# Two blocks of attention and feed-forward: first loads on ScalarE's queue, warm matmuls, and a reordered handover between stages

## The reference

```
x = x + fake_quant(layernorm(x)) @ fake_quant(ctx)   # per batch; 8-bit grid, q1 @ q2
x = x + mx_linear(silu(mx_linear(h, w_gate)) * mx_linear(h, w_up), w_down)   # h = layernorm(x)
x = x + attention(layernorm(x), ctx, ctx, wq, wk, wv, wo)  # 32 query heads, 8 key heads, rope
x = x + ffn(layernorm(x), gate_w, up_w, down_w)            # silu(gate) * up, down
```

## Time and profile before

| | us |
|---|---|
| median of 3 runs | 683.79 |
| lowest, highest | 683.26, 684.01 |
| profiled execution | 685.39 |
| its span, first to last instruction | 683.6 |
| TensorE busy | 661.1 |
| VectorE busy | 516.4 |
| GpSimd busy | 474.2 |
| ScalarE busy | 347.5 |

### The profile page before, as it was taken

How to read it: one execution, slowest core, us unless ns; L and a number is a source line. 1 busy time by engine, 2 the same in 40 slices (tenths; PEclk the granted TensorE clock), 3 DMA queues, 4 the chain that set the end, 5 groups by cost and what they waited for, 6 DMA issues and landing times.

```text
span 683.6 us, 10829 instructions
## 1 busy us (share of the span) xinstructions
PE 661.1 (97%) x3004; PEld 486.5 (71%) x3004; DVE 516.4 (76%) x1024; ACT 347.5 (51%) x667; POOL 474.2 (69%) x435
## 2 busy tenths in 40 slices
PE   6999999999899999999999999999999998999997
PEld 2344444446667888888888888888888776888886
DVE  5999897986788888888888888888888886621113
ACT  2686324424656656656666666666556653221111
POOL 0688958334698788787787787797688477076661
PEclk9999999999999999999999999999999999999999
DMA  8999775403322222232231131131233012013311
GB/s 317 390 328 245 230 198 133 155 1 121 94 78 78 63 85 70 61 89 64 61 99 54 61 105 48 61 107 46 61 94 121 17 32 92 1 48 102 111 63 62
DMA packets 59147, 72.63 MB, mean 106 GB/s; under 512 B 23152, under 2 KB 31472, under 8 KB 58096
## 3 DMA queue, kind: packets, MB, share of 16 engines
q1 hardware_dynamic: 59120, 72.31, 34.5%
HBM read 58.00 MB, written 9.44 MB: 99 GB/s over the span
## 4 chain that ended last, share of the span: by engine, by line
PE 67%; DVE 14%; POOL 8%; issue 7%; ACT 2%; DMA 1%; SPq 1%; DVEq 0%; ACTq 0%; POOLq 0%
PE ps L683 14%; PE ps L685 14%; PE ps L684 14%; PE ps L751 10%; PE ps L716 6%; PE ps L568 3%; PE ps L542 3%; POOL mx_raw L1148 2%; DMA mx_raw<-in_mxw 1%; DVE ps L1578 1%; PE ps L604 1%; POOL mx_w L1157 1%; DVE mx_amax L1406 1%; POOL prob L1220 1%; DVE stats L1319 1%
## 5 line engine op out<-in xcount | busy, mean ns | idle before, releaser
L1220 POOL TENSOR_SCALAR prob<-prob,rinv 128x512 f32<-128x512 f32 x128 | 90.0, 703 | 73.6 <-DVE rinv L1585 73.5
L1046 ACT ACTIVATE prob<-ps,nmax 128x512 f32<-128x512 f32 x128 | 88.5, 691 | 97.2 <-DVE nmax L1578 96.8
L751 PE MATMUL ps<-xt,wq_sb 128*128 128x512 f32 x384 | 103.2, 393 | 3.6 <-DVE q_cos L1593 2.1
L1057 ACT CAST pT<-ps 128x512 fp32r<-128x512 f32 x128 | 75.2, 588 | 53.0 <-PE ps L716 51.9
L1578 DVE CUSTOM_DVE_ANT_0 ps<-ps,mask_sb 128x512 f32<-128x512 f32 x128 | 88.0, 687 | 6.6 <-PE ps L685 6.1
L1599 DVE TENSOR_TENSOR pT<-ps,pT 128x512 fp32r<-128x512 f32 x128 | 86.5, 675 | 3.0 <-ACT pT L1057 2.0
L751 PEld LDWEIGHTS ps<-xt,wq_sb 128*128 128x128 f32 x384 | 71.6, 188 | 22.3 <-issue 4.9
L716 PE MATMUL ps<-idf,prob 128*128 128x128 f32 x512 | 76.8, 272 | 0.4 <-POOL prob L1220 0.3
L716 PEld LDWEIGHTS ps<-idf,prob 128*128 128x128 f32 x512 | 63.6, 140 | 17.8 <-POOL prob L1220 1.6
L683 PE MATMUL ps<-pT,vt 128*128 128x512 f32 x128 | 60.8, 475 | 0.6 <-DVE pT L1599 0.5
L542 PE MATMUL ps<-ctxT,wk_sb 128*128 128x512 f32 x128 | 58.0, 594 | 0.4 <-ACT v_st L892 0.4
(11 more groups left out here) (179 smaller groups left out, 1548.0 us busy)
## 6 DMA issues: line engine op xcount, KB each, us to landing
mx_raw<-in_mxw SPq DMA_DIRECT2D x8, 1024.0 KB, 8.1
wq_raw<-in_wq SPq DMA_DIRECT2D x32, 256.0 KB, 3.2
wo_raw<-in_wo SPq DMA_DIRECT2D x32, 256.0 KB, 2.7
v_scr<-v_st SPq DMA_DIRECT2D x16, 256.0 KB, 3.7
k_scr<-k_st SPq DMA_DIRECT2D x16, 256.0 KB, 3.5
kr<-k_scr SPq DMA_DIRECT2D x16, 256.0 KB, 2.8
kr_swp<-k_scr SPq DMA_DIRECT2D x32, 128.0 KB, 3.4
vr<-v_scr SPq DMA_DIRECT2D x16, 256.0 KB, 3.3
```

Of the source, the lines that this page charges most:

```text
L751: last = mm(query_bank(H), wq_sb[:, par, l, k], xt[:, r, k], start=(n == 0), stop=(n == 11))
L1046: nc.scalar.activation(prob[:, j], bank(j % 2), ACT.Exp, bias=nmax[:, j:j + 1], scale=-1.0, accum_out=rsum[:, j:j + 1]).then_inc(exps, 1)
L1057: copy(pT[:, v % 2, 0, :, i * P:(i + 1) * P], bank(2 + i % 2).rearrange("p (k c) -> p k c", k=4)).then_inc(ph_ready, 1)
L1220: nc.gpsimd.tensor_scalar(prob[:, i], prob[:, i], rinv[:, i:i + 1], 1.0, ALU.mult, ALU.mult).then_inc(probs, 1)
```

## The change

- ScalarE's queue issues the four slices, the first key weights, the rest of the context columns and the second half of the value weights, ahead of its other work. SyncE's queue keeps X, the MX chunks, context rows and all later DMAs.
- TensorE runs eight matmuls of ones (bf16, 512 columns) into the first value bank before `first_values`.
- ScalarE copies the first two value banks before the lifts of chunk 0, and rounds the rows after them.
- The rotation, addition, copy and low part of the two first keys are moved: key 0 behind the MX work on GpSimd and behind the quantisation of the inter products on VectorE, key 1 behind the first steps of query head 0.
- GpSimd splits the weights of heads 2 and 3 in step 0 of units -2 and -1, before the rotation of a query, instead of in step 1.
- Head 3 goes to bank 7, and heads 3 and 4 wait for one rotated head fewer.
- The last late key unit is computed as one quarter before the second stage and three quarters in unit -1, instead of two halves in units -2 and -1.
- `last_low` stands after the first step of `standardise` instead of after five.

The diff, without context lines:

```diff
@@ -62,6 +62,8 @@
+WARM = 8
@@ -112,7 +114,7 @@
-            return bank(7 if isinstance(head, int) and head == 1 else 6)
+            return bank(7 if isinstance(head, int) and head in (1, 3) else 6)
@@ -335,10 +337,6 @@
-            def slice_load(k):
-                sp.dma_start(ctxT[:, k, 0:CTX], ctx_cols[k * P:(k + 1) * P, 0:CTX]).then_inc(ctxT0_in[k], 16)
-                sp.dma_start(wv_sb[:, k, 0:512], wv[k * P:(k + 1) * P, 0:512]).then_inc(wv0_in[k], 16)
@@ -363,20 +361,13 @@
-            slice_load(0)
-            slice_load(1)
-            slice_load(2)
-            slice_load(3)
-            k_load(0)
-            sp.dma_start(ctxT[:, :, CTX:CTOK], ctx_cols[:, CTX:CTOK].rearrange("(k p) c -> p k c", p=P)).then_inc(ctxT1_in, 16)
-            sp.dma_start(wv_sb[:, :, 512:1024], wv[:, 512:1024].rearrange("(k p) c -> p k c", p=P)).then_inc(wv1_in, 16)
@@ -543,6 +534,12 @@
+            def keep_busy():
+                pe.wait_ge(consts_ready, 1)
+                for _ in range(WARM):
+                    mm(bank(rotating(STEPS[0][0][0])), ones[:], ones[:].unsqueeze(1).to_broadcast([P, 4, P]), start=True, stop=True)
@@ -579,6 +576,7 @@
+            keep_busy()
@@ -686,6 +684,7 @@
+            late_keys(4, range(0, 1))
@@ -739,8 +738,7 @@
-                    first = isinstance(H, int) and H <= 2
-                    after(pe, q_cosed, H // 2 if first else H)
+                    after(pe, q_cosed, H - 1 if isinstance(H, int) and H <= 4 else H)
@@ -779,8 +777,8 @@
-                    if isinstance(U, int) and U in (-2, -1) and j == 3:
-                        late_keys(4, range(2 * U + 4, 2 * U + 6))
+                    if isinstance(U, int) and U == -1 and j == 3:
+                        late_keys(4, range(1, 4))
@@ -904,6 +902,9 @@
+            def rows_round():
+                rows = xhat[:].rearrange("p t d -> p (t d)")
@@ -934,11 +935,18 @@
+            for k in range(KD):
+                act.dma_start(ctxT[:, k, 0:CTX], ctx_cols[k * P:(k + 1) * P, 0:CTX]).then_inc(ctxT0_in[k], 16)
+                act.dma_start(wv_sb[:, k, 0:512], wv[k * P:(k + 1) * P, 0:512]).then_inc(wv0_in[k], 16)
+            act.dma_start(wk_sb[:, 0], wk[0]).then_inc(wk_in[0], 16)
+            act.dma_start(ctxT[:, :, CTX:CTOK], ctx_cols[:, CTX:CTOK].rearrange("(k p) c -> p k c", p=P)).then_inc(ctxT1_in, 16)
+            act.dma_start(wv_sb[:, :, 512:1024], wv[:, 512:1024].rearrange("(k p) c -> p k c", p=P)).then_inc(wv1_in, 16)
+            copy_values(0, 0)
+            copy_values(1, 0)
-            copy_values(0, 0)
-            copy_values(1, 0)
+            rows_round()
@@ -1008,9 +1016,11 @@
+            def first_key_high(b):
+                act.wait_ge(key_roped, b + 1)
+                copy(kt[:, 0, b], kr[:, b]).then_inc(kh_ready, 1)
-            act.wait_ge(key_roped, 1)
-            copy(kt[:, 0, 0], kr[:, 0]).then_inc(kh_ready, 1)
@@ -1022,6 +1032,7 @@
+            first_key_high(0)
@@ -1030,8 +1041,6 @@
-            act.wait_ge(key_roped, 2)
-            copy(kt[:, 0, 1], kr[:, 1]).then_inc(kh_ready, 1)
@@ -1065,6 +1074,8 @@
+                        if isinstance(U, int) and H == 0:
+                            first_key_high(1)
@@ -1188,14 +1199,12 @@
-                    pool.wait_ge(rk_in, 16)
-                    pool.wait_ge(ln_ready, 2 * NT)
-                    first_key_rotate(0)
+            pool.wait_ge(rk_in, 16)
-            first_key_rotate(1)
+            first_key_rotate(0)
@@ -1210,6 +1219,13 @@
+            def query_split(U, u, g):
+                H, par = U + 4, u % 2
+                if within(H, NH):
+                    pool.wait_ge(wq_in[par], 16 * (g * 2 + (u + 4) // 2 + 1))
+                    after(pool, q_sums, H - 1)
+                    split(wq_sb[:, par, 0], wq_sb[:, par, 1], wq_raw[:, par], wqh_ready, wq_split, H + 1)
@@ -1218,16 +1234,16 @@
+                    if isinstance(U, int) and U in (-2, -1) and j == 0:
+                        query_split(U, u, g)
-                    if j == 1 and within(U + 4, NH):
-                        H, par = U + 4, u
-                        load = g * 2 + (u + 4) // 2 + 1
-                        pool.wait_ge(wq_in[par % 2], 16 * load)
-                        after(pool, q_sums, H - 1)
-                        split(wq_sb[:, par % 2, 0], wq_sb[:, par % 2, 1], wq_raw[:, par % 2], wqh_ready, wq_split, H + 1)
+                    if j == 1 and not (isinstance(U, int) and U in (-2, -1)):
+                        query_split(U, u, g)
+                    if isinstance(U, int) and U == -3 and j == 1:
+                        first_key_rotate(1)
@@ -1332,6 +1348,8 @@
+                if between:
+                    between()
@@ -1339,8 +1357,6 @@
-                    if n == 1 and between:
-                        between()
@@ -1524,13 +1540,13 @@
-            first_key_add(0)
+            first_key_add(0)
@@ -1553,10 +1569,9 @@
-            first_key_add(1)
-            first_key_low(1)
+            first_key_add(1)
@@ -1592,6 +1607,8 @@
+                        if isinstance(U, int) and H == 0:
+                            first_key_low(1)
```

## The result

The changed kernel takes **685.73 us** (median of 8 executions, 685.50 to 686.46) against 683.75 (8 executions of the kernel before on the same chip): a ratio of 1.0031, 95% interval 1.0022 to 1.0039. It is slower by 2.0 us, where the prediction said 2.0 faster (681.8).

The account below looks back on a forecast made before the run. TensorE, busy 661.1 of 683.6 us, bounds the kernel, with VectorE's MX chain limiting the first 77 us. Terms -0.7 + 0.9 + 0.9 + 0.9 = 2.0 us take 683.79 to 681.8; eight-in-ten range 679.9 to 684.2.

Parts of the forecast that it names:

- Part A: 0 to 77 us: loads on ScalarE's queue, warm matmuls, new ScalarE order; -0.7 us (a loss), bounds -2.0 and +1.0.
- even split: First 20 us: the two queues share bytes evenly, so slice 3 lands at 13.3 us.
- Rival 2: First 20 us: queues share four to one, slice 3 at 19.2, lifts late; -2.0 for -0.7, 683.1 us; chance 0.27.
- The forecast for the second chunk: First 20 us: the second MX chunk, third on SyncE's queue, lands at 18.55 us, 0.4 later than 18.17.
- The term of better filling: First 20 us: a second queue issuing beside the first wins back 0.7 us, ends 0 and 1.3.
- The mark set for being wrong: First rounding over 1 us from 20.9 us, or GpSimd or ScalarE turning the removed query waits into equal ones.
- the 0.55 charged for half clock before L532: Near 66 us: TensorE waits 3 to 4 us, then runs at 1.2 GHz; 0.55 us more loss than the chain alone.
- the 1.7 us that the ones were to save: Start of the slices: matmuls of ones spare the lengthening of the first four records, about 1.7 us.
- Part C: 110 to 157 us: first key addition leaves VectorE's path ahead of the third product; +0.9 us, bounds 0 and 1.47.
- Part D: 157 to 216 us: second key, late keys, weight splits and query bank edits remove waits; +0.9 us, bounds 0.3 and 3.5.
- Part E: Around 580 us: last_low runs 0.79 us earlier, so TensorE starts its projections sooner; +0.9 us, bounds 0.5 and 1.3.
- rival 3: First 25 us: ScalarE's queue is served last, slice 3 at 22.0, copy and lift 4.8 late; 685.9 us; chance 0.09.

Follow-up runs that it names:

- e1: Changed kernel with ScalarE's first two MX lifts ahead of the two value copies again: 684.19 us, ratio 0.9999.
- e4: Kernel before, unchanged, measured and profiled once more: median 684.24 us, profile span 682.0.
- e5: Changed kernel with the first three MX chunks each loaded by four DMAs of 2 KB rows instead of one of 8 KB rows: 687.12 us, ratio 1.0044.
- e2: Changed kernel with the loads issued by SyncE's queue again in the old order, copies still before lifts: 684.31 us, ratio 0.9998.
- e6: e1 with the weight splits for heads 2 and 3 behind the rotation of the queries on GpSimd again: 686.24 us, ratio 1.0026.
- e7: Changed kernel with loads on SyncE's queue and lifts ahead of copies again, all else kept: 683.59 us, ratio 0.9995.
- e10: Kernel before plus the first key's later addition, rotation and copy, the earlier last_low and the matmuls of ones: 685.88 us, ratio 1.0022.
- e12: e1 with ScalarE issuing slices 1 to 3 only once the second row tile of X has landed: 690.06 us.
- e9: Kernel before with only head 3's query sum in bank 7 and the matching wait value: 683.82 us, ratio 0.9989.
- e17: Kernel before with head 3's bank and wait value, earlier last_low, splits of heads 2 and 3 first, and a late-key quarter early: 683.25 us, ratio 0.9988.
- e3: Kernel before with only the queue changed, ScalarE issuing the eleven loads: 685.31 us, ratio 1.0011.
- e8: e7 with the last half of the attention output added after the first Newton step again: 684.42 us against 683.59.
- e11: e7 without the eight matmuls of ones: 683.81 us, ratio 0.9994.
- e16: Changed kernel, unchanged, measured again: 685.94 us, ratio 1.0027.
- e15: Kernel before with head 3's bank and wait value, earlier last_low, and a quarter of the late key matmuls before the first query: 684.46 us, ratio 1.0008.

## Why the prediction was wrong, by its own steps

**Part A, -0.7 forecast (in the direction of faster: a loss of 0.7), 2.7 lost.** The step that failed is "With an even split of bytes, slice 3 lands when 2 x 2.1 = 4.2 MB are down", at 13.3 us. Rows are shared one for one, 361 to 361, and so bytes one to four; slice 3 was there at 19.7. With that fell the next clause, that the two copies fit ahead of the lifts "and nothing is added": the copies ended at 22.34 and the lifts stood behind them, which e1 shows to be 1.7 of the 2.7 us. Rival 2 had this mechanism with its mark (slice 3 at 19.2) and its consequence (lifts behind the copies). The Trainium skill, "DMA: Bandwidth & Descriptors", section "Queues, rings and completion order", says turns are taken packet by packet; by that rule, with a row as the packet, rival 2 was the likelier case, and the trace agrees.

Rival 2's own size was 2.0, 0.7 short of the measured 2.7: slice 3 came 0.5 us later than its 19.2, and the first sum was ready 1.1 us behind it in place of 0.9, so that the second copy ended at 22.34 in place of 21.5. With the order undone 1.0 us of the loss is left (e1). That is a step that the prediction never had: X's rows too share one for one with the slices. X's last statistics ended at 10.41 in place of 9.18, and the peak search began at 14.87 where e4 and before have 13.79 and 13.63. In the changed kernel this lies hidden behind the copies.

The forecast for the second chunk, "18.55 us, 0.4 us later than 18.17", would have failed with an even split too. It sets a time from the formula beside a time from the trace. The same formula puts that chunk of the kernel before (X, four slices, two chunks: 5.25 MB) at 20 - (6.6 - 5.25)/0.40 = 16.6 us, where it landed at 18.17. Formula against formula the delay is 2 us, and in e5, which has the even split, the chunk landed at 21.53, 3.4 us later than before.

The term of better filling, 0.7 us, was close: 0.22 MB more by 20 us, at 0.40 MB per us, are 0.55 us. The prediction worked out that it would be nothing by the Trainium skill, "DMA: Bandwidth & Descriptors", section "Issuing engines are not separate DMA queues". The traces don't agree with that working. The section itself says that a second issuing engine saves only the time on the sequencer, and a gain at the very start fits that: 274 GB/s in the first 10 us in place of 254. It just did not go to the loads that the chain waits for.

The prediction also took the second chunk for the only limit of the first rounding because VectorE waited 2.03 us for it. The other one, GpSimd's scaling until 16.56 + 3.78 = 20.34, ended 0.1 us before the peak search on that chunk did (18.17 + 2.29), in the same group of rows. The mark set for being wrong, a first rounding over 1 us from 20.9, was met.

**Matmuls of ones.** It was right that TensorE gains nothing before 77 us. But the 0.55 charged for half clock before L532 did not occur: the wait there was 1.32 us, not 3 to 4. And the 1.7 us that the ones were to save on the first matmuls came in six of the ten profiles with them (e1, e2, e6, e7, e10 and e12 start at 0.43 to 0.52 us from one record to the next) and not in the other four, the changed kernel's two among them (0.83 to 0.99 for the first four or five).

**Part C, +0.9; about 0.4 measured**, within the bounds 0 and 1.47. The mechanism was right and the size was not: what TensorE could get back was its own wait of 0.47 us for that product, not the 1.47 us of the addition.

**Part D, +0.9; 0.0 to 0.3.** That both waits for the query bank go was right, as was that the next limit is close behind. The mark of a first softmax 0.4 us earlier was missed (13.56 us behind the first query, 13.52 before). The clause of the prediction on ScalarE or GpSimd turning them into equal waits came true: 3.5 us for `prob`. Mis-sized was the gain that gets through: the bank alone is worth 0.6 to 1.0 (e9), and the whole part nearly nothing. The second key's copy, addition and rotation, counted as hidden in gaps, are the likely reason (e17, 0.6), which no run shows alone.

**Part E, +0.9; -0.1, or 0.8 where half clock is spared.** The wait before L683 fell from 2.15 to 1.48, as forecast. The failing step is that the projections end "when the normalised rows are ready (582.54 + 1.0)", a time taken from the rows of before: these rows wait for the addition too, since both stand on VectorE (timeline of the changed kernel, TensorE, 582 to 586 us):

```profile
582.39 0.50 PE L681 MATMUL ps<-wo_sb,oT 128*128 128x512 f32 x1 [1.48 <-DVE oT L1663]
...
585.27 0.98 PE L806 MATMUL ps<-idf,xhat 128*128 128x128 f32 x7 [1.22 <-DVE xhat L1364]
```

**The base.** The profile of before was an execution 1.6 us above its median; three stages' excess was in it, and C and E were costed from just those rows.

**The rivals.** The time lies beside rival 3's 685.9, but its mechanism did not occur: neither queue went first. That the numbers meet is chance. Rival 2's condition held, and with its -2.0 a time of 683.1 would have followed; the other 2.6 us are the 0.7 by which it mis-sized its own mechanism and gains of C, D and E that did not come (1.9 by this difference; 2.2 by the table of stages, where 0.5 of 2.7 came).

## What to carry to other kernels

Two loaded queues share by rows, not by bytes: moving short-row loads to a second queue delays them and everything short-rowed on the first, and helps only the long rows (the second chunk was there by 17.48, where VectorE had waited for it until 18.17). Compare a time worked out by a formula with what the same formula gives for the kernel before, not with a time from the trace. Before counting a wait as a gain, find the second limit behind it in the same rows (here 0.1 us behind the chunk, 0.4 behind the addition in e4), and profile the kernel twice: what differs between two profiles of one kernel is not there to be won. A copy that waits for a late load should stand behind, not ahead of, the work that another engine is waiting for; the order alone cost 1.7 us.

## What the runs showed of the hardware

- Half clock (0.50 to 0.52 in the records, 1.2 GHz) follows some idle stretches of TensorE of 1.9 to 2.2 us in some executions and not in others of the same kernel: behind 2.15 us at 580 in before, e3, e8 and e9 and not in e4; behind 1.9 us for `prob` in e5, e7, e8, e11, e12 and e16 and not in after, e1 and e2; nor behind 2.60 us for weights in e6, but behind 2.16 in e15. No profile has it behind a shorter wait in mid-kernel, the longest of which are 1.85 us (e5, at 69.56), 1.68 (e10) and 1.48 (every kernel with E). By the stages it cost 0.9 to 1.3 us where TensorE was the limit (stage E, 7.85 to 8.23 for 6.94; of e8's 1.3 the last stage gave back 0.6, 91.84 for 92.44) and 0.3 where it was not (stage D).
- The first matmuls of the slices run at half the usual rate in all nine profiles without matmuls of ones (0.81 to 0.99 us from one to the next in place of 0.43, for the first three to five). With eight matmuls of ones at 1.01 to 4.61 us they do so in four profiles of ten. The changed kernel and e6 are a pair in which it differs, although both start on the slices at 5.61 us and their lists for TensorE and the loads up to there are the same. No run shows why.
- An exponent instruction of 64 elements on VectorE took 0.20 us before (20.49) and 1.82 after (19.81), while GpSimd scaled a chunk until 21.57; in e1, e7 and e2 it was 1.82, 0.56 and 0.35 and ended within 0.1 us of GpSimd's instruction each time. GpSimd scales a chunk by two instructions; the exponent always ended with the second, beside which it had started. The peak search before it, beside the first, kept its 2.29 us. The Trainium skill, "Trainium Architecture — The Big Picture", section "What this means for kernel authors", states that VectorE and GpSimd contend for a port pair by an exclusive lock; by that rule a small instruction can wait out a long one, and the traces agree. No run here tests it.
- ScalarE's last issue in the changed kernel held it for 3.27 us (6.23 to 9.5), in front of its table load. Nothing waited for it.
